# Graph kernel on one core: start-up order, TensorE's branch and the encoder's second products

## The reference

```python
# layer 0: y = elu(norm(x) @ W_root + b + sum_r mean over edges of type r of norm(x)[src] @ W_rel[r])
x = layernorm(x + x + y @ wo)
# layer 1
h = relu(layernorm(x) @ W1 + b1) @ W2 + b2            # the encoder, 1024 -> 512 -> 256
for i in range(3):
    z = h + segment_sum(h[src], dst)
    z = relu(z @ Wa[i] + ba[i]) @ Wb[i] + bb[i]
    h = h + relu(layernorm(z))
x = layernorm(x + layernorm(x + relu(h @ Wd1 + bd1) @ Wd2 + bd2))
```

## Time and profile before

| | |
|---|---|
| median of three runs | 589.47 us |
| the profiled execution | 590.16 us |
| its span, first to last instruction | 588.3 us |
| TensorE busy | 572.2 us (97%) |
| VectorE busy | 385.1 us (65%) |
| ScalarE busy | 223.7 us (38%) |
| mean granted TensorE clock | 0.994 |

### The profile page before, as it was taken

How to read it: one execution, slowest core, us unless ns; L and a number is a source line. 1 busy time by engine, 2 the same in 40 slices (tenths; PEclk the granted TensorE clock), 3 DMA queues, 4 the chain that set the end, 5 groups by cost and what they waited for, 6 DMA issues and landing times.

```text
span 588.3 us, 8363 instructions
## 1 busy us (share of the span) xinstructions
PE 572.2 (97%) x2584; PEld 396.1 (67%) x2584; DVE 385.1 (65%) x1000; ACT 223.7 (38%) x457; POOL 88.6 (15%) x70
## 2 busy tenths in 40 slices
PE   8999999999999999999999999999999999999992
PEld 4555555555577677675888888877877867455541
DVE  7598999888847888889503330018848657756455
ACT  5454344432213546553412221012223134276555
POOL 3000000000000000003065513401202230042230
PEclk9999999999999999999999999999999999999997
DMA  9510011111031112128300000600100100021123
GB/s 267 145 36 9 28 35 35 35 35 35 0 84 44 35 42 66 35 78 218 138 36 0 0 0 1 213 11 2 37 1 0 36 1 0 2 70 44 62 70 105
DMA packets 20871, 30.74 MB, mean 52 GB/s; under 512 B 5428, under 2 KB 15254, under 8 KB 20838
## 3 DMA queue, kind: packets, MB, share of 16 engines
q1 hardware_dynamic: 20422, 29.66, 17.1%
q10 hardware_dynamic: 416, 0.67, 0.4%
HBM read 25.20 MB, written 5.12 MB: 52 GB/s over the span
## 4 chain that ended last, share of the span: by engine, by line
PE 88%; DVE 4%; issue 2%; DVEq 2%; DMA 2%; ACT 1%; POOL 0%; SPq 0%
PE banks L736 16%; PE banks L935 12%; PE banks L1021 12%; PE banks L855 12%; PE banks L825 5%; PE banks L722 5%; PE banks L957 4%; PE banks L947 4%; PE banks L884 4%; PE banks L886 4%; PE banks L865 3%; PE banks L1011 3%; PE banks L829 2%; DVEq L1176 1%; PE banks L840 1%
## 5 line engine op out<-in xcount | busy, mean ns | idle before, releaser
L736 PE MATMUL banks<-w_all,xnT 128*125 128x429 f32 x320 | 130.3, 531 | 0.4 <-DMA w_all<-in_L_gnn_W_rel 0.4
L736 PEld LDWEIGHTS banks<-w_all,xnT 128*125 128x125 f32 x320 | 54.7, 190 | 30.7 <-issue 29.5
L1194 DVE TENSOR_TENSOR adj<-adj,banks 125x220 f32 x160 | 60.9, 381 | 17.5 <-PE banks L722 17.0
L855 PE MATMUL banks<-hT,w_s 128*128 128x250 f32 x320 | 68.7, 375 | 0.2
L855 PEld LDWEIGHTS banks<-hT,w_s 128*128 128x128 f32 x320 | 60.3, 190 | 8.9 <-issue 2.0
L884 PE MATMUL banks<-y_hi,adj 125*125 125x288 f32 x200 | 55.3, 304 | 0.6 <-issue 0.6
L722 PEld LDWEIGHTS banks<-oh_code,oh_low 125*128 125x128 bf16 x320 | 30.5, 97 | 35.1 <-issue 29.7
L886 PE MATMUL banks<-y_lo,adj 125*125 125x286 f32 x200 | 53.6, 295 | 0.0
L1340 DVE TENSOR_SCALAR hT<-banks,g_c,b_c 128x125 f32<-128x125 f32 x60 | 19.4, 400 | 45.1 <-PE banks L840 45.1
L1166 DVE TENSOR_TENSOR oh_code<-iota_c,edge 125x880 bf16<-125x880 f16 x80 | 48.9, 611 | 0.0
L935 PE MATMUL banks<-adj,h_hi 125*128 125x250 f32 (+1 forms) x180 | 48.2, 367 | 0.0
(11 more groups left out here) (205 smaller groups left out, 878.3 us busy)
## 6 DMA issues: line engine op xcount, KB each, us to landing
xt<-in_x SPq DMA_DIRECT2D x15, 448.0 KB
out_x<-ot SPq DMA_DIRECT2D x9, 448.0 KB
w_s<-in_L_gnn_W SPq DMA_DIRECT2D x5, 512.0 KB, 6.1
xn<-in_x SPq DMA_DIRECT2D x5, 448.0 KB
wd_s<-in_L_gnn_Wd SPq DMA_DIRECT2D x1, 2048.0 KB, 13.7
w_all<-in_L_gnn_W_rel SPq DMA_DIRECT2D x6, 286.0 KB, 7.0
wo_s<-in_L_gnn_wo_weight SPq DMA_DIRECT2D x1, 1024.0 KB, 6.5
w_all<-in_L_gnn_W_root SPq DMA_DIRECT2D x3, 286.0 KB, 6.6
```

What stands on the lines that cost most here:

```text
L736: ins = pe.matmul(pb[0:P, 2 + 2 * v + n, 0:FH], xnT[:, u], w_all[:, u, n * FH:(n + 1) * FH], start=(u == 0), stop=(u == KD - 1))
L855: ins = pe.matmul(pb[:, 4 + f % 2, 0:2 * P], w1_s[:, k, f * 128:(f + 1) * 128], hT[:, k], start=(k == 0), stop=(k == KD - 1))
L1194: dve.tensor_tensor(cols, cols, window(b, q), ALU.add).then_inc(done, 1)
```

## The change

Five places change. (1) x of tile 0 comes as the left half of its 112 rows, the 13 rows, and the right half of the 112 rows, with a semaphore `x_left` for the first two. (2) SP carries src behind the first weight piece and typ behind the second; ACT carries lnw8 and dst. (3) PE runs nine products of zeros at first, and two more between the turns of the left and the right half; the edge codes are turned one block earlier (3 and 4). (4) PE's branches test `fine` and hold the usual path first; the step into the encoder stands inside both bodies. (5) In `chunk_of_3` the second products of k = 0..2 of both tiles come first, then the wait for the last block of `r1T`, then k = 3 of both.

```diff
-            load_x(0, 0)
-            sp.dma_start(lnw8[:], ...).then_inc(lnw_in, 16)
-            for q in range(len(PIECES)):
+            many, few = row_parts
+            sp.dma_start(x_of(0)[many, 0:512], x_t[0][many, 0:512]).then_inc(x_left, 16)
+            sp.dma_start(x_of(0)[few], x_t[0][few]).then_inc(x_left, 16)
+            sp.dma_start(x_of(0)[many, 512:D], x_t[0][many, 512:D]).then_inc(xs_in[0], 16)
+            load_w(sp, 0)
+            sp.dma_start(src_i[:], src.rearrange("(g e) -> g e", g=G)).then_inc(src_in, 16)
+            load_w(sp, 1)
+            sp.dma_start(typ_i[:], typ.rearrange("(g e) -> g e", g=G)).then_inc(typ_in, 16)
+            for q in range(2, len(PIECES)):
                 load_w(sp, q)
@@ ScalarE
+                if t == 0:
+                    act.wait_ge(x_left, 32)
                 act.wait_ge(xs_in[v], 32)
...
-            for a, d, done in ((dst_i, dst, dst_in), (src_i, src, src_in), (typ_i, typ, typ_in)):
-                act.dma_start(a[:], d.rearrange("(g e) -> g e", g=G)).then_inc(done, 16)
+            act.dma_start(lnw8[:], ...).then_inc(lnw_in, 16)
+            act.dma_start(dst_i[:], ...).then_inc(dst_in, 16)
@@ TensorE, start
-            warm(7, 5)
+            pe.sem_inc(xs_in[0], 16)
+            warm(9, 5)
             ...
+            pe.wait_ge(x_left, 32)
+            turn(0, 0)
+            warm(2, 5)
             pe.wait_ge(xs_in[0], 32)
-            turn(0, 0)
             turn(1, 0)
             warm(2, 5)
...
-                if u == 4:
+                if u == 3:
                     pe.wait_ge(lows_ready, 1)
                     turn_edges(0, e_low)
-                if u == 5:
+                if u == 4:
                     pe.wait_ge(edges_ready, 1)
@@ TensorE, branch (aggregate's branch is turned round in the same way)
-            with pe.If(big > 0):
-                ... counts, relations(F32, adj_x)
-            with pe.Else():
-                pe.wait_ge(adj_done, 1)
-                relations(F32R, adj)
-            pe.wait_ge(pre_elu, T)
-            turn_elu(T - 1)
-            turn_chunk(0)
-            project(T - 1)
+            with pe.If(fine > 0):
+                pe.wait_ge(adj_done, 1)
+                relations(F32R, adj)
+                into_encoder()
+            with pe.Else():
+                ... counts, relations(F32, adj_x)
+                into_encoder()
@@ TensorE, encoder
-                pe.wait_ge(r1_done, 1 + c * K1 + K1)
+                pe.wait_ge(r1_done, 1 + c * K1 + K1 - 1)
                 pe.wait_ge(w2_in, 16)
                 pe.wait_ge(h_done, 1 + c * 2)
                 for u in range(2):
-                    for k in range(K1):
-                        ins = pe.matmul(...)
-                    ins.then_inc(h_mm, 1)
+                    for k in range(K1 - 1):
+                        to_h(u, k)
+                pe.wait_ge(r1_done, 1 + c * K1 + K1)
+                for u in range(2):
+                    to_h(u, K1 - 1).then_inc(h_mm, 1)
```

More of the change, by code:

```diff
@@ L183, in graph_kernel @@
         src_in, dst_in, typ_in = sem("src_in"), sem("dst_in"), sem("typ_in")
-        x_even, x_odd = sem("x_even"), sem("x_odd")
+        x_even, x_odd, x_left = sem("x_even"), sem("x_odd"), sem("x_left")
         xs_in = (x_even, x_odd)
@@ L269, in load_x @@
                     sp.dma_start(x_of(v)[rows], x_t[t][rows]).then_inc(xs_in[v], 16)
-            load_x(0, 0)
-            sp.dma_start(lnw8[:], ln_w.rearrange("(k p) -> k p", p=128)).then_inc(lnw_in, 16)
-            for q in range(len(PIECES)):
+            many, few = row_parts
[7 more added lines that the diff above has]
+            for q in range(2, len(PIECES)):
                 load_w(sp, q)
@@ L469, in _ @@
             act.activation(small1[:, 6:7], eps0[:, 0:1], ACT.Sqrt)
-            for a, d, done in ((dst_i, dst, dst_in), (src_i, src, src_in), (typ_i, typ, typ_in)):
-                act.dma_start(a[:], d.rearrange("(g e) -> g e", g=G)).then_inc(done, 16)
+            act.dma_start(lnw8[:], ln_w.rearrange("(k p) -> k p", p=128)).then_inc(lnw_in, 16)
+            act.dma_start(dst_i[:], dst.rearrange("(g e) -> g e", g=G)).then_inc(dst_in, 16)
             act.wait_ge(lnw_ps, 1)
@@ L808, in _ @@
             pe.wait_ge(big_ready, 1)
-            big = pe.value_load(bign[0:1, 0:1], min_val=0, max_val=1)
+            fine = pe.value_load(bign[0:1, 1:2], min_val=0, max_val=1)
             tile_of_1(T - 1, 1, (T - 2) * UG, 0, G - (T - 2) * UG, None)
@@ L857, in chunk_of_3, with to_h @@
                     ins.then_inc(r1_mm, 1)
+                def to_h(u, k):
+                    return pe.matmul(pb[0:P, 6 + u, 0:HB], r1T[:, k, u * P:(u + 1) * P], w2_s[:, k],
+                                     start=(k == 0), stop=(k == K1 - 1))
                 if not last:
                     turn_chunk(c + 1)
-                pe.wait_ge(r1_done, 1 + c * K1 + K1)
+                pe.wait_ge(r1_done, 1 + c * K1 + K1 - 1)
                 pe.wait_ge(w2_in, 16)
@@ L863, in chunk_of_3 @@
                 for u in range(2):
-                    for k in range(K1):
-                        ins = pe.matmul(pb[0:P, 6 + u, 0:HB], r1T[:, k, u * P:(u + 1) * P], w2_s[:, k],
-                                        start=(k == 0), stop=(k == K1 - 1))
-                    ins.then_inc(h_mm, 1)
+                    for k in range(K1 - 1):
[3 more added lines that the diff above has]
+                    to_h(u, K1 - 1).then_inc(h_mm, 1)
             def relations(kind, a):
@@ L895, in _, with into_encoder @@
             pe.wait_ge(y_split, 1 + T)
-            with pe.If(big > 0):
+            def into_encoder():
+                pe.wait_ge(pre_elu, T)
+                turn_elu(T - 1)
+                turn_chunk(0)
+                project(T - 1)
+            with pe.If(fine > 0):
[3 more added lines that the diff above has]
+            with pe.Else():
                 with pe.Fori(0, NW * G) as i:
@@ L938, in aggregate @@
                         if s_last and f == K2 - 1 and part is h_lo:
+                            ins.then_inc(z_mm, 1)
+                with pe.Else():
+                    for c, (c0, n) in enumerate(CH):
+                        for f in range(K2):
+                            ins = pe.matmul(pb[:, 3 * f + c, 0:n], h[:, s, f * 128:(f + 1) * 128],
+                                            adj_x[:, 0, s, c0:c0 + n], start=(s == 0), stop=(s == T - 1))
+                        if s == T - 1:
                             ins.then_inc(z_mm, 1)
```

## The result

The changed kernel takes 592.59 us (median of seven runs, 591.52 to 595.26) beside 590.22 us for the kernel before in the same runs: ratio 1.0047, 95% interval 1.0033 to 1.0061. By the ratio it is slower by 2.8 us (1.9 to 3.6) where I forecast faster by 0.95 us. The two medians lie only 2.4 us apart: the ratio is not their quotient. The runs of the kernel before spread from 589.29 to 591.06 us, and the median of a few of them falls anywhere in between.

What follows compares the result with a forecast made beforehand. TensorE was taken as the bound, busy 572.2 of 588.3 us. Terms -0.25 (start), 0 (branch), 0 (jump) and -0.7 (encoder) summed to -0.95: 589.47 to 588.5 us, range 587.3 to 589.5.

Steps and rivals of the forecast that it cites:

- The new jump: Jump ending the usual body, behind the last `project`: 2.4 us fetch covered by 4.7 us of products; term 0, worst +2.4.
- Rival (c): Jump into the encoder not covered: fetch ends near 277.4, first product 1.5 us late, 590.0 us; chance 0.06.
- Start, the clock: At tile 0: without PE's pauses the clock is up by its start, eight records take 2.93 us; two to one.
- Start, the weights: Ahead of block 2: third weight piece still lands at 12.5 and limits the gain; term -0.25 us, ends -0.9 and +0.5.
- TensorE's branch: Ahead of the second stage: 0.64 us idle goes but becomes a longer wait for the bias; term 0, ends -0.64 and 0.
- Encoder: Last chunk's second products: six of eight hide the last relu, removing the idle time; term -0.7 us, ends -0.7 and -0.5.
- Rival (d): The encoder's edit does nothing, as its second wait stops the six products being handed out in time: 589.2; chance 0.04.
- (a): Start: clock rises no earlier, tile 0 starts half a microsecond late; +0.25 instead of -0.25, 589.0 us; chance 0.22.
- (b): More comes through: third weight piece early, -0.9, bias sooner, -0.4, with the encoder's -0.7: 587.5 us; chance 0.18.

Runs made afterwards that it cites:

- branch_only: The kernel before with only TensorE's branches turned round and the encoder step inside both bodies: 592.73 us, ratio 1.0046.
- quiet_fetch: The changed kernel with SP holding back all but the first piece of the encoder's weights, last tile's x ahead of them: 590.34 us, ratio 1.0005.
- padded_jump: The changed kernel with seven more products, results unused, between `project` and the jump: 594.92 us, ratio 1.0084.
- branch_back: The changed kernel with TensorE's branches put back, step into the encoder once behind the branch: 589.42 us, ratio 0.9985.
- encoder_only: The kernel before with only the encoder's second products in two steps: 589.23 us, ratio 0.9989.
- edges_later: The changed kernel with branches put back, src and typ issued behind the third weight piece, edge codes turned at blocks 4 and 5: 588.84 us, ratio 0.9976.
- start_only: The kernel before with only the start's edits: 590.19 us, ratio 1.0002.
- step_outside: The changed kernel with the step into the encoder once, behind the branch, so the usual body ends before it: 590.15 us, ratio 1.0005.
- short_else: The changed kernel without the work of the unusual branch body, so almost no code is jumped over: 591.08 us, ratio 1.0021.
- short_else_x: The changed kernel without the unusual branch body's work and with the last tile's x one weight piece earlier: 589.73 us, ratio 0.9994.

## Why the prediction was wrong

**The new jump: this step failed.** "Its price uncovered is from the packet at about 167.8 to 170.24, 2.4 us. Its cover: PE has twelve records from 271.23 to 275.92 to do, 4.7 us ... Term 0, worst end +2.4." Rival (c), at a chance of 0.06 and 590.0 us, named the mechanism, and two of its numbers came close: the packet near 275 (274.5 to 275.0), the first product 1.5 us late (1.58 in branch_only, 1.89 in the profiled run). Four sizes were off:

- The cover. I took the whole 4.7 us. Ahead of this jump the packet never moved that early: 1.0 to 1.6 us ahead of PE's end in the changed kernel, 2.6 to 3.1 in quiet_fetch, 3.6 to 4.1 in padded_jump. One reason stands in the order of PE: its last wait ahead of the jump, for GpSimd's `xh`, ends only at 270.44 us, as the changed kernel's chain of waits shows below. Only from there can the sequencer go on to the jump, over twenty records. The packet followed 2.5 to 3.0 us after the end of that wait in quiet_fetch (270.50 there) and 4.1 to 4.6 us after it in the changed kernel. How long the sequencer needs for twenty records, no run varies.
- The fetch. I read its price in the earlier trace rows, a quiet stretch, with 16 GB/s, and carried it to the fullest one in this part of the kernel, with 295 GB/s. From the time when quiet_fetch shows the jump already reached (273.0 to 273.5) to the first product at 277.94 it is 4.4 to 4.9 us, not 2.4. From the packet itself to that product it is 2.9 to 3.4 us.
- The clock. An idle time of 1.6 to 1.9 us brought the half clock behind it: 1.68 us in branch_only, 2.9 in the profiled run. The sum had no such term, though the first part of the prediction had just read a low clock behind pauses in the start.
- The next code page. The jump's packet is followed by a second one 3 to 5 us later, read here as the page behind the target: 1.38 us idle in the profiled run, 0.45 in quiet_fetch, none in branch_only and padded_jump.

```profile
267.78 2.66 POOL xh L381 x2
270.44 0.04 issue
270.49 1.07 PE banks L851 x8
```

Together: 1.58 + 1.68 = 3.26 us in branch_only's profiled execution, 2.7 us (1.9 to 3.5) by its ratio. The worst end of +2.4 was too small for both, though the interval reaches below it. For the whole change that end gave -0.95 + 2.4 = +1.45 us, and +2.8 us (1.9 to 3.6) were measured.

The Trainium skill, page Runtime: NRT & Kernel Launch, section Instruction fetch mechanics, says that a taken branch outside the held pages must wait for a fetch; the idle time of 1.58 and 1.89 us ahead of the encoder agrees with it. The prediction had that rule and set it aside for the cover.

**Start, the clock: right, the reason not shown.** It was up before tile 0, even earlier than forecast, and so it was in every profiled kernel with the new start. But of the three profiled kernels with the old start one, branch_only, had it up by then too. There PE waited 1.46 us ahead of tile 0 and made the eight records at the full level, where the kernel before took 4.70 us:

```profile
9.12 3.12 PE L736 MATMUL banks<-w_all,xnT 128*125 128x429 f32 x8 [1.46 <-DMA w_all<-in_L_gnn_W_rel]
```

So that the pauses held the clock down before, as I had it, is not shown. The timeline of the changed kernel answers to the earlier trace rows:

```profile
2.30 3.45 PE L777 MATMUL banks<-oh_code 125*128 125x440 bf16 x9 [2.30 <-DVE oh_code L1099]
5.68 0.22 PE L784 MATMUL banks<-ident,lnw 8*128 8x8 f32 x1
...
7.99 1.68 PE L744 MATMUL banks<-w_all,xnT 128*125 128x429 f32 x4 [0.34 <-DMA w_all<-in_L_gnn_W_rel]
...
10.22 1.71 PE L744 MATMUL banks<-w_all,xnT 128*125 128x429 f32 x4 [0.56 <-DMA w_all<-in_L_gnn_W_rel]
...
13.15 0.44 PE L802 MATMUL banks<-ident,bounds 80*1 80x80 f32 x4 [1.22 <-DMA w_all<-in_L_gnn_W_rel]
13.43 1.65 PE L744 MATMUL banks<-w_all,xnT 128*125 128x429 f32 x4
```

The norm's weight is in time (5.68 without idle, 5.7 forecast; in branch_back it holds PE for 0.2), and tile 0 starts at 7.99 where I had 8.9, since the turned blocks already ran faster.

**Start, the weights: the wait right, the landing wrong.** That PE would end up waiting for the third piece was right. That the piece would land at 12.5 "unchanged", its later issue "covered by the backlog", was not. PE waits for the first three pieces, 2.1 us in all, and in all nine profiled kernels with this start block 2 begins at 12.92 to 13.37 us behind a wait of 1.2 to 1.3 us for the piece. With the old start it had landed by 12.58 us in the kernel before and by 12.49 in branch_only, 0.3 to 0.9 us sooner (in encoder_only PE itself came later, at 13.47). SP issues the piece a microsecond later, first the kernel before, then the changed one:

```profile
4.91 0.61 SPq L256 DMA_DIRECT2D w_all<-in_L_gnn_W_root  x1
```

```profile
5.86 0.43 SPq L256 DMA_DIRECT2D w_all<-in_L_gnn_W_root  x1
```

and src and typ now stand ahead of it in its own queue. Which of the two moved the landing, no run separates; edges_later undoes both, with src and typ behind the piece instead of on the other queue, and block 2 begins at 12.04. The term of -0.25 us came out at 0 (start_only, 1.0002, -0.5 to +0.7 us): what the faster clock gives, the later weights take.

**TensorE's branch: right.** L901 now starts at 169.43 without idle time (170.24), and L828's weight load at 180.32 after 1.25 us instead of 0.33 (180.14). The 0.64 us became a longer wait for the bias: 1.0 us at L828 in the list of waits, and I had said 0.9.

**Encoder: right.** The 0.56 us of the earlier trace rows are gone. In encoder_only:

```profile
365.38 3.62 PE L860 MATMUL banks<-w_s,r1T 128*125 128x256 f32 x16
...
368.64 0.92 PE L941 MATMUL banks<-adj,h_hi 125*128 125x250 f32 x3
```

The aggregation follows at once, and the ratio of 0.9989 is 0.6 us, 0.7 forecast, though its interval just touches 1. Rival (d) falls.

**The other rivals.** (a) falls with the clock, though a start that gains nothing, as it had it, is nearer to what was measured than my -0.25; (b) falls with the landing of the third piece. Without the branch edits the change measures 0.9985, that is 0.9 us faster where the sum without the jump said 0.95. That they meet so closely is in part luck: the start gave 0 instead of -0.25 and the encoder -0.6, and the interval of 0.9985 is -0.3 to -1.4 us.

## What to carry to other kernels

Turning a branch so that the usual path comes first does not take the jump away; it moves it to the end of the usual body, so look at what stands there: PE's work in hand, how full the DMA engines are at that time, and what the clock does after a stop. Take the price of a fetch from a stretch with the same DMA load, add the clock's fall (it came behind the stops of 1.58 and 1.89 us ahead of the encoder), and look for the last wait in the engine's order ahead of the jump: only what stands behind it is cover. Here 4.7 us of work in the last `project` did not cover the fetch among full DMAs, and 6.1 us more behind it did; with quiet DMAs the same `project` covered it. A stop saved ahead of a transfer that is late anyway is worth nothing until the transfer is earlier: the start began to gain only when the weights went out ahead of the edges.

## What the hardware showed that I had not expected

Code packets and data seem to delay each other. With full DMA engines (about 260 to 320 GB/s) the jump's packet moved 1 to 2 us later than in the quiet case (274.5 to 275.0 against 273.0 to 273.5), and a 16 KB packet that moved between 267 and 275 us went with a last tile of x landing 1.33 to 1.85 us late for DVE in four kernels (changed 1.33, branch_only 1.40, step_outside 1.47, short_else 1.85). In the kernel before, branch_back and padded_jump, with no such packet in that stretch, DVE did not wait for x. padded_jump's packet, in a stretch with 301 GB/s, moved early enough ahead of PE all the same. In quiet_fetch packets moved there too and DVE did not wait, but x, issued at the same time, had one weight piece less ahead of it. The row of the changed kernel:

```profile
277.33 1.22 DVE L1320 SCALAR_TENSOR_TENSOR xt<-xt,banks 125x1024 f32<-125x1024 f32 x1 [1.33 <-DMA xt<-in_x]
```

That the packet is the cause of the late x is an inference from which kernels show it; issuing x earlier cured the wait in short_else_x, which it would do for any cause. In the profiled run of the changed kernel the clock fell after an idle time of 1.89 us, in branch_only after 1.58 us; the wait of 1.22 us at L802, in the start of the same execution, was followed by four products in 1.65 us, and in branch_only a wait of 1.46 us at L736 by eight in 3.12 us, both the full level.
